# Hybrid attention and mixture-of-experts block: a later rank for the second FFN's additions, fetches and stores

## What is computed

```python
x = x + _L0_attn_a_ref(_layernorm(x, axis=-1), ...)   # causal attention, 16 heads, 4 groups
x = x + _L0_ffn_ref(_layernorm(x, axis=-1), ...)      # 8 experts, the best 2 of each row
x = x + _L0_attn_b_ref(_layernorm(x, axis=-1), ...)   # attention to 4 memory banks
x = x + _L0_ffn_ref(_layernorm(x, axis=-1), ...)      # the same experts again
```

```python
h = jax.nn.silu(g) * u
y = jnp.einsum('besi,eih->besh', h, Wd)
out = jnp.einsum('bse,besh->bsh', combine.astype(x.dtype), y)
```

## Time and profile before

| what | us |
|---|---|
| three runs | 531.47, 535.22, 540.63 |
| their median | 535.22 |
| the profiled execution | 536.22 |
| its span in the trace | 534.4 |

### The profile page before, as it was taken

How to read it: one execution, slowest core, us unless ns; L and a number is a source line. 1 busy time by engine, 2 the same in 40 slices (tenths; PEclk the granted TensorE clock), 3 DMA queues, 4 the chain that set the end, 5 groups by cost and what they waited for, 6 DMA issues and landing times.

```text
span 534.4 us, 10902 instructions
## 1 busy us (share of the span) xinstructions
PE 483.7 (91%) x3346; PEld 327.6 (61%) x3346; DVE 373.3 (70%) x1098; ACT 269.3 (50%) x642; POOL 248.5 (46%) x308
## 2 busy tenths in 40 slices
PE   5799899999999999989999979999979998999960
PEld 2335555665665666766777636675757776677740
DVE  4799989879999966664445647868868684344473
ACT  3578898877887784423333425524223532334320
POOL 5408519338850062373433555446473756233330
PEclk8789999999999999999999999999989999799995
DMA  8254510111120232454335392102151457233484
GB/s 278 114 198 206 165 35 8 56 41 61 61 84 19 84 129 78 122 187 140 95 113 158 76 191 41 37 34 81 41 155 43 141 158 209 80 101 107 161 295 165
DMA packets 43736, 60.77 MB, mean 114 GB/s; under 512 B 5856, under 2 KB 38240, under 8 KB 43040
## 3 DMA queue, kind: packets, MB, share of 16 engines
q1 hardware_dynamic: 33696, 38.24, 23.0%
q0 software_dynamic: 9984, 21.83, 13.6%
HBM read 28.89 MB, written 25.00 MB: 101 GB/s over the span
## 4 chain that ended last, share of the span: by engine, by line
PE 58%; DVE 10%; DMA 5%; issue 4%; ACT 2%; POOL 2%; SPq 1%; POOLq 0%; DVEq 0%; ACTq 0%
PE PS L1138 15%; PE PS L1155 10%; PE PS L1184 4%; PE PS L1025 3%; PE PS L1119 3%; PE PS L1147 3%; PE PS L1002 3%; PE PS L1193 3%; PE PS L1087 2%; PE PS L1201 2%; DMA ys<-yo,xin 2%; DVE smax L1477 2%; PE PS L1165 2%; PE PS L1076 2%; DMA kbd<-ys 2%
## 5 line engine op out<-in xcount | busy, mean ns | idle before, releaser
L1876 POOL DMA_INDIRECT ys<-yo,xin x78 | 75.4, 966 | 107.3 <-DVE yo L1698 97.6
L1138 PE MATMUL PS<-wexp,xTt 128*128 x312 | 106.8, 470 | 2.2 <-issue 1.3
L1477 DVE TENSOR_REDUCE smax<-PS 128x1 f32<-128x512 f32 (+3 forms) x176 | 102.3, 633 | 6.1 <-PE PS L1004 5.6
L1303 ACT ACTIVATE prob<-PS 128x512 f16<-128x512 f32 (+1 forms) x176 | 92.7, 562 | 20.1 <-PE PS L1027 18.2
L1861 POOL DMA_INDIRECT xs<-xn,pos x64 | 62.5, 977 | 57.9 <-DVE pos L1572 40.8
L1155 PE MATMUL PS<-wexp,hT 88*128 x312 | 81.3, 388 | 2.3 <-ACT hT L1353 2.1
L1138 PEld LDWEIGHTS PS<-wexp,xTt 128*128 128x128 f32 x312 | 55.6, 192 | 25.1 <-issue 5.2
L1685 DVE SCALAR_TENSOR_TENSOR sg<-th,PS 128x176 f32<-128x176 f32 x78 | 26.2, 336 | 61.6 <-ACT th L1347 61.3
L1347 ACT ACTIVATE th<-PS 128x176 f32<-128x176 f32 x78 | 24.7, 317 | 83.9 <-PE PS L1138 83.9
L1155 PEld LDWEIGHTS PS<-wexp,hT 88*128 88x128 f32 x312 | 55.9, 191 | 15.2 <-issue 4.2
L1025 PE MATMUL PS<-qT,kbd 128*128 128x512 f16 (+3 forms) x256 | 60.8, 300 | 2.2 <-ACT qT L1295 1.0
(11 more groups left out here) (210 smaller groups left out, 836.7 us busy)
## 6 DMA issues: line engine op xcount, KB each, us to landing
xin<-xs SPq DMA_DIRECT2D x78, 129.0 KB, 2.1
kbd<-ys SPq DMA_DIRECT2D x20, 256.0 KB, 4.3
wexp<-in_experts SPq DMA_DIRECT2D x4, 1216.0 KB, 9.1
xs<-zeros SPq DMA_DIRECT2D x32, 129.0 KB
xn<-xn SPq DMA_DIRECT2D x8, 512.0 KB, 3.3
xall<-ys POOLq DMA_DIRECT2D x6, 512.0 KB, 6.8
out<-xall SPq DMA_DIRECT2D x8, 256.0 KB, 2.7
kbd<-kT SPq DMA_DIRECT2D x60, 32.0 KB, 1.9
```

The costliest lines, as they stand in the source:

```text
L1138: mm = pe.matmul(PS[:, bank, 0:2 * FI], xTt[:, j % NXT, kc * P:(kc + 1) * P], wexp[:, bass.ds(expert[f, j], 1), kc * 2 * FI:(kc + 1) * 2 * FI]
L1303: act.activation(prob[:, u % NPR, 0:nr * w], PS[:, bank, 0:nr * w], ACT.Exp, scale=ATT_SCALE)\
L1477: dve.tensor_reduce(smax[:, i, REP * g + r0:REP * g + r0 + nr], PS[:, bank, 0:nr * w].rearrange("p (r w) -> p r w", r=nr), AX.X, ALU.max). ...
L1876: pool.indirect_dma_start(ys[f], bass.IndirectOffsetOnAxis(xin[:, j % NXIN, D + 1:D + 2].bitcast(I32), axis=0), yo[:, j % NYO], None).then ...
```

## The change

Two ranks are raised, by one `TILES` (39) each: that of the second FFN's `combine`, which hands it to the fetches on SP and to the additions on VectorE, and that of the stores on SP. The additions of batch b now have `last + 117 + b`. The row product of the last tile, 38, has `last + 120`, its gate product `last + 114`.

```diff
     for b in range(B):
-        combine(w, 1, b, last + 2 * TILES + b)
+        combine(w, 1, b, last + 3 * TILES + b)
         for h in range(2):
-            w.add(SP, last + 2 * TILES + b + 0.5, 0.4, "store", b, h, after=[(DVE, "join", 1, b, h)], lands=2.8)
+            w.add(SP, last + 3 * TILES + b + 0.5, 0.4, "store", b, h, after=[(DVE, "join", 1, b, h)], lands=2.8)
```

## The result

| | before | changed |
|---|---|---|
| median of 20 runs each | 538.30 us | 539.74 us |
| fastest and slowest | 531.47, 543.51 | 535.59, 542.87 |
| mean | 538.35 | 539.40 |
| ratio of changed to before | | 1.0059 (95%: 1.0035 to 1.0084) |
| span of the profiled execution | 534.4 | 537.6 |

The ratio is that of the medians of the runs that lie within 1.5% of their own kernel's fastest, which leaves out the eight slowest of the twenty of before (median of the rest 536.57) and none of the changed kernel's. The time is within my range, and within 2%. But by the interval the kernel has become slower by 0.6%, some 3 us, where I had forecast 0.8 us. The two traces too differ by 3.2 us. So the question for the experiments was where 3 us come from.

The account below looks back on a forecast made before the run. The end was taken as set by the last row store, its landing and SP's queue, not TensorE. The rush ending 1.2 - 0.4 = 0.8 us later took the median from 535.2 to 536.0 us, range 531.5 to 540.5.

Parts of the forecast that it names:

- Tiles: VectorE's steps for the last tiles, additions moved between them: last row store at 519.05 us, before 519.18, gaining 0.1 us.
- the load ahead of the fetches: On SP, tile 38's load goes ahead of four transfers: the fetches behind it land about 0.4 us later.
- SP's queue: SP's stores and fetches behind later additions: fetch of batch 2's second half leaves at 517.8 us, before 516.29.
- The last row store in the rush: Tile 38's row store lands with the busy DMA stretch near the end, 0.8 us later, at 524.2 instead of 523.43.
- What lands when: DMA near the end: the rush begins 1.2 us later, loses one 0.4 us row store, and ends 0.8 us later.
- the quiet price: Lower bound for the last row store's landing: 2.54 us, as for a row store with quiet DMA, landing at 521.6.
- The second rival: Output store between batch 3's fetches waits for its addition and decides the end: 536.4 to 536.9 us; chance 0.25.
- Third rival: VectorE and SP hold four additions back until the tiles are done, delaying batch 2's fetches: about 538 us; chance 0.05.
- My sum: End of the span: 0.8 us later, 535.2 instead of 534.4; as a median 536.0 us.
- How the numbers follow: Chances and range: forecast 0.45, within 2% 0.97; range 531.5 to 540.5 us from the scatter of earlier runs.

Follow-up runs that it names:

- n5: The changed kernel run a fourth time with no edit; ratio to before 0.9954, median 581 us.
- n2: The changed kernel run a second time with no edit; ratio to before 0.9989, median 585 us.
- n3: The changed kernel run a third time with no edit; ratio to before 0.9966, median 578 us.
- n6: The changed kernel run a fifth time with no edit; ratio to before 1.0002, median 540 us.
- e4: The changed kernel with three fetches of batches 2 and 3 moved ahead of output stores on SP; ratio to before 0.9931, median 579 us.
- e8: The kernel of e4 run a second time with no edit; ratio to before 0.9948, median 577 us.
- e10: The kernel of e4 run a third time with no edit; ratio to before 0.9950, median 537 us.
- e9: The changed kernel with batch 2's second fetch moved behind batch 3's first on SP; ratio to before 1.0070.
- e3: The changed kernel with the four additions of batches 0 and 1 behind tile 38's row product on VectorE; ratio to before 1.0123.
- n1: The kernel before run a second time with no edit; ratio 0.9999, median 587 us.
- e1: The kernel before with only tile 38's load moved ahead of the fetches on SP; ratio to before 1.0007.
- e7: The kernel of e4 with batch 1's first-half addition behind tile 35's row product and its second-half addition behind tile 38 on VectorE; ratio to before 0.9993.
- n4: The kernel before run a third time with no edit; ratio 1.0008, median 541 us.

## Why the prediction was right or wrong

**Tiles: right.** VectorE's steps came as worked out up to the later data: tile 34's row product 1.5 us after tile 35's gate product began, then two additions, two gate products, tile 35's row product. The last row store was forecast at T + 15.6 and came at T + 15.66, and in the repeats at 15.02, 15.86 and 15.68 (18.89 in n5). That it hit to 0.04 us is in part luck: the addition began 0.4 us later than forecast (T + 7.0 for 6.6), and the steps behind it took 8.66 us where my steps add up to 9.05. The 0.1 us of gain is the 1.5 us saved behind the addition, less the 1.4 by which the addition came later. I had counted 0.4 us for the load ahead of the fetches; the addition's data came 1.4 later than in the first trace of before, and this term was too small in that trace. TensorE stood 1.05 us for tile 36's gate product, not 0.6.

**SP's queue: right.** Batch 2's second fetch was forecast at T + 14.4 and came at T + 14.31, and in the repeats at 13.67, 14.52 and 14.34 (17.54 in n5).

**The last row store in the rush: right in kind, too large.** The step "*What lands when*" took the rush 0.8 us later and the row store with it; this is the term of the sum that was too large. From the last row store to batch 3's fetch it was 4.67 us instead of 5.3, against 4.39 before, and 4.3 to 4.5 in n2, n3 and n6. That SP's transfers hold the store up is supported by e4, e8, e10 and e9; that moving them by 1.45 us moves its landing as far is not so: the fetch that took 6.0 us before took less, and its addition began 0.6 us later (T + 19.86 instead of 19.26). Where batch 2's fetches leave sooner, in e4, e8 and e10, the row store lands in 2.64 to 3.03 us, near the quiet price of 2.54. The Trainium skill (DMA: Bandwidth & Descriptors, section "Anatomy of one DMA"), by whose figures I had estimated 2.3 us, comes near that and not near the 4.05 to 4.34 us in the rush.

**The second rival took part.** The chain runs through the output store between batch 3's fetches, which waits for its addition; it decided by 0.1 us, and by 0 to 0.4 in the repeats, not by 1.2. By its own steps its time ends at 535.2 + 1.5 = 536.7 us, not at 536.9.

**Third rival: its size was wrong**, as e3 shows: counted from before, 6.6 us for 3. Of the 7.8 us by which batch 2's fetch came later 1.2 were hidden, where I had 4 of 7.3.

**The total.** My sum gave +0.8 us for the tail. The traces had +0.2, and as a mean over three and five executions the tail is unchanged (31.4 and 31.3): the 0.8 us of the step "*What lands when*" didn't come. Against the measured ratio of 1.0059 my forecast of 1.0015 is wrong all the same. The step that failed there is the last one, "*How the numbers follow*": I put what lies ahead of the last 30 us at nothing, and took the scatter of the runs as something that only widens the range of the time, and not as something from which a difference clear of its interval can come. In its place the runs showed 3.02 of the traces' 3.2 us ahead of T, T apart by as much as 5.9 us on one chip with one list up to it, and four repeated ratios from 0.9954 to 1.0002. Whether a part of the 0.6% below 0.2% is real can't be told from these runs. That the time fell into my range says little, since the range was that scatter.

## What to carry to other kernels

Before two traces are compared, find the last instruction that the change can't have moved, and measure from it: here that turned 3.2 us into 0.2, and after it distances like 10.17 and 8.65 us repeat to the hundredth in all traces but one, while whole executions of one kernel scatter by several us. In a queue that takes its steps in order, put fetches that others will have to wait for ahead of output stores for which nobody waits, above all where they would otherwise fall on a transfer on which the end hangs: this gave 0.5 to 0.7% against the kernel before, when a reordering by rank that only swapped who waits gave nothing. A tile's work that gets ahead of an addition gains only if the other engines' lists let the next step follow: neither VectorE's list nor the other three alone gave the 1.5 us that they gave together.

## What the runs showed of the hardware

**A wait of TensorE can cost more than itself.** n5 is the one changed execution with a long tail (583.12 us, among twelve from 573.80 to 586.53). Batch 1's data came at T + 8.56, and TensorE waited 2.60 us for tile 36's gate product, against 1.05 in the first changed trace. Its timeline, and the stretches (columns as in the earlier trace rows):

```profile
558.88 0.42 PE L1147 MATMUL PS<-first_rows,hf 128*88 128x128 f32 x2 [2.60 <-DVE hf L1689]
559.13 2.63 PE L1138 MATMUL PS<-wexp,xTt 128*128 x4
```
```profile
558.00:560.00 2.00, 1.12 (x4) 0.80 (x5) 1.93 (x7) 0.38 (x1) 0.00 (x0) 0.80 0.51 183
560.00:562.00 2.00, 2.00 (x7) 1.08 (x6) 1.13 (x2) 0.20 (x1) 1.16 (x1) 0.50 0.14 46
562.00:564.00 2.00, 2.00 (x9) 1.69 (x9) 1.30 (x4) 0.50 (x2) 0.00 (x0) 0.84 0.97 295
```

The granted clock fell to 0.50 (1.2 GHz) behind the wait, tile 38's first product took 2.63 us where it took 1.44 in the first changed trace and 1.35 before, both at a granted clock of 1.00, and the distance to the last row store became 10.33 instead of 8.65. It may be that the changed list leaves TensorE more exposed to late data, but only two executions speak for it: in n1 the addition came 1.26 us later than in the first trace of before and the tail grew by 1.1; in n5 it came 1.56 later than in the first changed trace and the tail grew by 1.9.

**An issue can stall.** In the first trace of before SP's fourth transfer of this stretch took 1.13 us to issue, where its neighbours took 0.36 to 0.46, and in the changed one the third took 1.33; both overlap GpSimd's row store of tile 32. The longest is in n6, whose T is 507.80 (a row of its chain):

```profile
507.64 2.25 SPq L913
```

Where the load left only with or after that row store (e1, e7, e8), the eight transfers were issued in 4.2 to 4.5 us instead of 4.7 to 5.9. But in n1 an issue that overlaps the same row store took no more than 0.49 us. No experiment was made on this alone, so the cause is open.

**Chips differ by 8%, by single waits.** One list takes about 540 us on some chips and 580 on others. n1 (580) had a granted clock of 0.91 from 120 to 300 us, and n4 (540), with the same list, 1.00. But most of the 47 us between their T aren't made by the clock. The chain of n1 has waits that n4's hasn't, put down by the profile to "another core or an unknown queue"; the longest is this one, and together they are 6.3% of the span, 37 us:

```profile
118.05 8.80 another core or an unknown queue
```

What is waited for isn't shown. The tail is about as long on both (n3 31.0, n6 30.9).
